# Gated window attention and router: attention product as fp32 32x32 tiles, mask on VectorE, shift on GpSimd, float32r router

## The reference

```python
q = Wq @ layernorm(x) + bq;  k = Wk @ ctx + bk;  v = Wv @ ctx + bv
dots = einsum('bhdt,bhdtw->bhtw', qh, k_win) * 32 ** -0.5   # keys t-8 .. t+7
out = einsum('bhtw,bhdtw->bhdt', softmax(dots), v_win)
x = x + tanh(g_xattn) * (Wo @ out + bo)
# router over the T axis: flat has 16*256 rows of 2048
scores = softmax(flat @ router_weight.T + router_bias)      # 64 experts
topk_w, topk_idx = top_k(scores, 8)
x = x + tanh(g_ffn) * (flat * topk_w.sum() + w_dense @ expert_bias)   # flat = layernorm(x)
```

## Time and profile before

| | us |
|---|---|
| median of 3 runs | 1553.32 (1553.09 to 1555.07) |
| the profiled execution, its own time | 1557.26 |
| its span, first to last instruction | 1555.1 |
| PE busy | 1464.6 (94%) |
| DVE busy | 1276.5 (82%) |
| ACT busy | 1144.8 (74%) |
| POOL busy | 1148.0 (74%) |

### The profile page before, as it was taken

One profiled execution on the slowest core, in us unless ns is written; L12 is line 12 of the kernel. 1 busy time (PEld: TensorE's weight loads), 2 busy tenths in 40 slices (PEclk: granted clock), 3 DMA queues, 4 the chain that ended last, 5 costly groups with the idle time before them and its releaser, 6 DMA issues.

```text
span 1555.1 us, 66658 instructions
## 1 busy us (share of the span) xinstructions
PE 1464.6 (94%) x28162; PEld 1199.9 (77%) x28162; DVE 1276.5 (82%) x2970; ACT 1144.8 (74%) x2009; POOL 1148.0 (74%) x1110
## 2 busy tenths in 40 slices
PE   4799999999999999999999999999999999999985
PEld 3687887888787888878788788878888887778764
DVE  5578987888898887988888898888889888788764
ACT  4687877777787877788787877778787787767652
POOL 4688777787777877877787887778778777677661
PEclk8899999999999999999999999999999999899896
DMA  7455455445546554454555545455554545434132
GB/s 230 125 140 126 106 173 131 123 149 143 147 121 172 141 131 146 121 157 128 149 149 141 156 119 159 128 146 147 144 159 114 159 132 142 121 98 128 44 81 85
DMA packets 365577, 210.39 MB, mean 135 GB/s; under 512 B 294497, under 2 KB 295521, under 8 KB 361057
## 3 DMA queue, kind: packets, MB, share of 16 engines
q1 hardware_dynamic: 365280, 206.14, 49.1%
HBM read 136.88 MB, written 33.55 MB: 110 GB/s over the span
## 4 chain that ended last, share of the span: by engine, by line
PE 46%; DVE 35%; issue 8%; POOL 5%; ACT 3%; DMA 2%; SPq 1%; POOLq 0%; DVEq 0%; ACTq 0%
PE ps_j L1117 18%; PE ps_s L1177 7%; PE ps_a L1142 6%; PE ps_r L1219 5%; DVE prob_t L900 5%; PE ps_s L1117 3%; DVE p_sum L890 3%; DVE st_x L907 2%; DVE wq_lo L822 2%; POOL prob L493 2%; DVE lg L1046 2%; DVE st_in L804 2%; DVE v_turn L871 2%; PE ps_s L1172 2%; PE ps_a L1196 2%
## 5 line engine op out<-in xcount | busy, mean ns | idle before, releaser
L486 POOL TENSOR_TENSOR score<-score,p_inv 128x384 f32<-128x384 f32 x256 | 221.6, 866 | 119.5 <-DVE p_inv L894 117.0
L493 POOL TENSOR_TENSOR prob<-score,prob 128x384 f16<-128x384 f32 x256 | 266.0, 1039 | 38.8 <-ACT prob L644 38.3
L1177 PEld LDWEIGHTS ps_s<-kv_win,q_col 32*32 32x32 f32 x16384 | 198.0, 107 | 57.8 <-issue 57.8
L1177 PE MATMUL ps_s<-kv_win,q_col 32*32 32x48 f32 x16384 | 234.1, 205 | 2.4 <-issue 2.2
L900 DVE STREAM_TRANSPOSE prob_t<-prob 128x512 f32<-128x512 f32 x256 | 176.7, 699 | 55.1 <-POOL prob L493 54.9
L467 POOL TENSOR_TENSOR c_lo<-c_in,c_hi 128x1024 fp32r<-128x1024 f32 x64 | 152.7, 2386 | 89.5 <-ACT c_hi L618 89.5
L1142 PEld LDWEIGHTS ps_a<-prob_t,v_diag 128*128 128x128 f16 x6528 | 175.3, 98 | 50.1 <-DVE prob_t L900 32.6
L1142 PE MATMUL ps_a<-prob_t,v_diag 128*128 128x48 f16 (+2 forms) x6528 | 187.6, 183 | 26.2 <-DVE prob_t L900 19.4
L462 POOL TENSOR_TENSOR att_lo<-att,att_hi 128x512 fp32r<-128x512 f32 x128 | 161.8, 1275 | 51.5 <-ACT att_hi L604 50.3
L1117 PE MATMUL ps_j<-c_hi,wkv_hi 128*128 128x512 f32 x512 | 171.3, 416 | 19.6 <-DVE kv_win L864 10.6
L890 DVE TENSOR_REDUCE p_sum<-score 128x8 f32<-128x384 f32 x256 | 139.2, 544 | 54.3 <-ACT score L638 53.6
(11 more groups left out here) (149 smaller groups left out, 3318.0 us busy)
## 6 DMA issues: line engine op xcount, KB each, us to landing
v_diag<-v_turn SPq DMA_DIRECT2D x512, 68.0 KB, 2.8
c_in<-ctx_dram SPq DMA_DIRECT2D x64, 512.0 KB, 4.9
x_in<-x_dram SPq DMA_DIRECT2D x64, 512.0 KB, 5.5
x_res<-x_dram SPq DMA_DIRECT2D x64, 512.0 KB, 4.3
out_dram<-x SPq DMA_DIRECT2D x32, 1024.0 KB, 7.0
c_sq<-ctx_dram SPq DMA_DIRECT2D x60, 512.0 KB, 5.5
x<-ctx_dram SPq DMA_DIRECT2D x4, 512.0 KB, 6.1
x<-experts_dram SPq DMA_DIRECT2D x2, 512.0 KB, 10.6
```

What stands on the lines that cost most here:

```text
L486: pool.tensor_tensor(score[:, u], score[:, u], p_inv[:, u, :].unsqueeze(2).to_broadcast([P, HALF, KEYS]), ALU.mult).then_inc(pm_rdy, 1)
L493: pool.tensor_tensor(part(prob[:, u % 2], 1)[:, :, 0:KEYS], score[:, u], part(prob[:, u % 2], 0)[:, :, 0:KEYS], ALU.subtract).then_inc(pl_ ...
L1177: ins = pe.matmul(s[head(h), n * KEYS:(n + 1) * KEYS], q_col[head(h), g, at:at + SUB], kv_win[c % 2][head(h), 0, g, at:at + KEYS], start=F ...
```

## The change

- **Attention product.** `attend` takes the turned values `v_turn` and `prob_t` directly, in fp32: for each of 17 blocks four matmuls on four 32x32 tiles, 68 for a group. `v_diag`, its DMAs, the fp16 halves (`high`, `low`, `values_low`) and the bound with its squares, loads and scales are gone. `v_turn` has two buffers.
- **Mask and shift.** The mask matmul is gone. VectorE adds the mask while it reads the scores from PSUM (`masked`), takes the maximum from SBUF, and GpSimd subtracts it (`shift`).
- **Router.** `wr_both` holds high and low part of the router weights as 128 float32r weight columns; the turned rows are split into `turn_hi` (ScalarE) and `turn_lo` (VectorE, `turned_low`) and are the moving operand, 256 columns. Once a sequence the sums are copied out (`logit_sums`), and two fp32 matmuls with `fold` add the halves and turn them back. `wd` and `lg` lie in PSUM.
- The low part of the scaled Wq moves from VectorE to GpSimd; the output is stored in four parts instead of one; the loads at the start stand in another order (no context squares, x ahead of the weights of the router and the experts); the order on each engine is another.

```diff
             def step(b, c, par):
-                if live(b, c, 0):
-
-                    turned, freed = nth(b, c, 0), nth(b, c, -1)
-                    for g in range(G):
-                        need(sp, vt_rdy[g], turned)
-                        need(sp, av_mm[g], freed)
-                        for h in range(HPG):
-                            sp.dma_start(v_diag[head(h), g, :, head(h)],
-                                         v_turn[head(h), g].rearrange("p (j d) -> p j d", d=SUB)).then_inc(vd_ld[g], 16)
...
-                def low(u):
-
-                    need(pool, ph_rdy, done(UNITS, b, c, 0, u))
-                    pool.tensor_tensor(part(prob[:, u % 2], 1)[:, :, 0:KEYS], score[:, u],
-                                       part(prob[:, u % 2], 0)[:, :, 0:KEYS], ALU.subtract).then_inc(pl_rdy, 1)
+                def shift(u, off):
+
+                    rows = score[:, u, :, 0:KEYS]
+                    need(pool, mx_rdy[u], nth(b, c, off))
+                    pool.tensor_tensor(rows, rows, neg_max[:, u, :].unsqueeze(2).to_broadcast([P, HALF, KEYS]),
+                                       ALU.add).then_inc(sh_rdy[u], 1)
...
+                def queries_weight_low():
+
+                    need(pool, wqh_rdy, b + 2)
+                    pool.tensor_tensor(wq_lo[:], wq_ln, wq_hi[:], ALU.subtract).then_inc(wql_rdy, 1)
...
-                def high(u):
-
-                    need(act, pm_rdy, done(UNITS, b, c, 0, u))
-                    need(act, pt_rdy, done(UNITS, b, c, 0, u - 2))
-                    act.activation(part(prob[:, u % 2], 0)[:, :, 0:KEYS], score[:, u], ACT.Copy).then_inc(ph_rdy, 1)
...
+                def logit_sums():
+
+                    need(act, r_mm, nth(b, c, -2))
+                    act.activation(acc[:], ps_r[:, ACC], ACT.Copy).then_inc(acc_rdy, 1)
...
-                def values_low(g):
-
-                    rows = kv_win[c % 2][:, 1, g, OWN]
-                    need(dve, vh_rdy[g], nth(b, c, 2))
-                    dve.scalar_tensor_tensor(part(rows, 1), ps_j[g][:], v_bias[parity(c, 2, par)][:, g:g + 1],
-                                             part(rows, 0), ALU.add, ALU.subtract).then_inc(vl_rdy[g], 1)
+                def masked(u, off):
+
+                    need(dve, s_mm[u], nth(b, c, off))
+                    need(dve, pt_rdy[u], nth(b, c, off - 1))
+                    dve.tensor_tensor(score[:, u, :, 0:KEYS], ps_s[u % 2][:, 0:HALF * KEYS].rearrange("p (n k) -> p n k", k=KEYS),
+                                      mask[:].unsqueeze(1).to_broadcast([P, HALF, KEYS]), ALU.add).then_inc(mk_rdy[u], 1)
...
+                def turned_low(g, off):
+
+                    need(dve, xth_rdy[g], nth(b, c, off))
+                    need(dve, r_mm, nth(b, c, off - 1))
+                    dve.tensor_tensor(turn_lo[:, :, g], ps_t[:].rearrange("p (k t) -> p k t", k=TB), turn_hi[:, :, g],
+                                      ALU.subtract).then_inc(xtl_rdy[g], 1)
...
-                        for n, (kv, kp) in enumerate(((0, 0), (1, 0), (0, 1))):
-                            ins = pe.matmul(ps_a[g][:, q0:q1], part(v_diag[:, g, j], kv),
-                                            part(prob_t[:, g, lo:hi], kp),
-                                            start=(j == 0 and n == 0), stop=(j == NB), skip_group_check=True)
+                        for h in range(HPG):
+                            ins = pe.matmul(ps_a[g][head(h), q0:q1], v_turn[(c + off) % 2][head(h), g, j * SUB:(j + 1) * SUB],
+                                            prob_t[head(h), g, lo:hi],
+                                            start=(j == 0), stop=(j == NB), skip_group_check=True)
...
-                    pe.matmul(s[:, 0:HALF * KEYS], ident_b[:], mask[:].rearrange("p n k -> p (n k)"),
-                              start=True, stop=False, skip_group_check=True)
...
                     for k in range(TB):
-                        for g in range(G):
-                            ins = pe.matmul(ps_r[:, g * E:(g + 1) * E], x1_t[:, g, k], wr[:, ch * TB + k],
-                                            start=(ch == 0 and k == 0 and g == 0),
-                                            stop=(ch == NCH - 1 and k == TB - 1), skip_group_check=True)
+                        for n, v in enumerate((turn_hi, turn_lo)):
+                            ins = pe.matmul(ps_r[:, ACC], wr_both[:, ch * TB + k], v[:, k].rearrange("p g c -> p (g c)"),
+                                            start=(ch == 0 and k == 0 and n == 0),
+                                            stop=(ch == NCH - 1 and k == TB - 1 and n == 1))
...
+                def fold_logits():
+
+                    need(pe, acc_rdy, b)
+                    if b == 1:
+                        need(pe, fold_rdy, 1)
+                    for g in range(G):
+                        ins = pe.matmul(wd[:, g], acc[:, g * P:(g + 1) * P], fold[:],
+                                        start=(g == 0), stop=(g == G - 1), skip_group_check=True)
+                    ins.then_inc(fo_mm, 1)
```

1117 lines of the change are left out of this document (511 added, 606 removed).

## The result

The changed kernel takes **1728.33 us** (median of 4, 1726.16 to 1730.52) where the kernel before takes 1554.01: a ratio of 1.1116, with a 95% interval of 1.1094 to 1.1138. It is 11% slower. The forecast was 1494 us. Of the cases in the prediction it is rival 5, instruction supply, which had 4% and a time of 1750.

What follows compares the result with a forecast made beforehand. PE, busy 94%, was taken to bound the kernel by the sum of its pieces; steps -28, late steps -12, start -18 and end -1 gave -59 from the 1553.32 median: 1494 us, range 1460 to 1540.

Steps and rivals of the forecast that it cites:

- rival 5: Instruction supply: PE gets only 74 instructions per us in the dense stretch; steps grow 4 us, total 1750; chance 4%.
- PE bounds the kernel, and its pieces can be summed: PE's pieces, summed start to start, set the time; a c = 0 step falls 0.66 us to 20.26.
- entry into the tiles: On PE, going from full matmuls to 32x32 tiles costs 0.08 us each time.
- The diagonal's 8 DMAs go, and nobody waits for them any more.: The eight DMAs a step that filled the diagonal disappear; no size was given.
- Rival 4: VectorE full at c = 1, late transposes, PE's clock falls; once per sequence +90, 1584 us; chance 10%.
- Late steps, -12 us: In steps like 57, VectorE's `nt_x` no longer meets GpSimd's `c_lo`; -12 us, bounds -14 and 0.
- Start, -18 us: Less data ahead of x: statistics end near 16, first queries at 25.5; -18 us, bounds -24 and -8.
- The end, -1,: At the kernel's end the last store is only a quarter; -1 us.
- VectorE and GpSimd below PE: VectorE falls from 1276 to 1229 us, below PE on the mean; GpSimd stays unchanged with 26% to spare.
- Wait for the output projection, 0.3 a step: Behind the second product PE has less cover and waits for `att_lo`; 0.3 us a step, between 0 and 0.58.

Runs made afterwards that it cites:

- e10: Changed kernel with the ctx load moved later in the step and the residual and stores ahead of the x load, nothing left out: 1606.34 us.
- e12: Changed kernel with the product reading only the upper 16 bits of values and probabilities, and its loads moved away from the dense part: 1481.00 us.
- e8: As e7, with one matmul a block in the product instead of three, low 16 bits left out: 1511.79 us.
- e7: Changed kernel with the product taken back to 51 full matmuls from the DMA-filled diagonal, low halves left out: 1499.03 us.
- e3: Changed kernel with the steady loads of ctx, x and the residual cut to 32 of 512 columns: 1608.75 us.
- e9: As e3, with one keys projection moved behind the next step's first product and one values projection ahead of the third scores unit: 1724.89 us.

## Why the prediction was wrong

- **PE bounds the kernel, and its pieces can be summed.** Right for the pieces, wrong as a bound. The product takes 1.52 us (828.25 to 829.77) where 1.72 was forecast: 11 ns a pass, not the 12.7 of the scores. The router starts at 835.60 and the scores at 836.75, 1.15 instead of 0.94 and 0.08 for the entry. The scores keep their 0.81. The entry into the tiles costs the 0.08 forecast: 0.54 from 855.48 to 856.02, of which the pair takes 0.46. The sum of the pieces was even 0.3 a step too high. But an undisturbed step hardly exists: the mean of 48 steps in the middle is 26.1 us against 22.9 before, where the forecast's (90.83 - 1.8) / 4 is 22.3; and the median with c = 0 is 25.7 against 20.9, where 20.3 to 20.7 was forecast.
- **The step that failed** is the first conclusion, that the time is set by the sum of PE's pieces: the supply of instructions stood in that sum at nothing. It was named as rival 5, priced at 4 us a step, 1750 in all, and given 4%. In its place the runs show 206 us more lost at blocks and 143 more at the lower clock. That the total comes so near to 1750 is in part luck: a mean step is 3.8 us above the forecast, but the rival knew only the rate of 74 per us, and with the loads out of the way (e10, 1606 us) a step is only 1.7 above it; the loads and the clock, which it left out, make up the rest. The only number beside the rival that speaks for its low chance is that the queue was busy for 1.0% of the time. That is the share of 16 engines' time that transfers take; it says nothing of how soon the next one can follow. 223 blocks in 1555 us are one in 7.0 us on the mean, and 256 instructions of the dense part, at 74 per us or more, need one in 3.5. The smallest distance between two transfers could have been taken from the trace of before: it is 3.28 us there. That one number would have shown that 74 per us is near a limit, and not only a rate that happened to be seen.
- **The page cited beside rival 5.** The Trainium skill (Runtime: NRT & Kernel Launch, Instruction fetch mechanics) gives PE a store of 2048 instructions and calls the cost of a block's boundary mostly hidden. The traces do not agree: when PE enters a block, never more than one further block of 256 has been transferred in any kernel here, and 225 us are lost at boundaries. The measurement decides. What the same section says of blocks of 256, and that the store is only two lines of 16 KiB, the traces bear out.
- **"The diagonal's 8 DMAs go, and nobody waits for them any more."** True, and the second miss. Nobody waited for them, but the ctx load stood behind them in SyncE's queue, and was late by it, 11.7 us into a step. Without them it runs beside the dense part. e10, which moves it back and the residual a little, takes 122 us back.
- **Rival 4, a fall of the clock**, came as a companion and not in the step with c = 1 alone: 233 us at the lower level instead of 90. Its own cause, the wait for the turned probabilities, did not come: 3.6 us are left of the 19.4 of the earlier trace rows.
- **Late steps, -12 us**: right in its mechanism. No `nt_x` was held by GpSimd; the mean of 48 equals the 161 ns of the free ones, where one took 2.20:

```profile
L719 DVE TENSOR_TENSOR nt_x<-nt_x,half_x 128x2 f32<-128x2 f32 x48 | 7.7, 161 | 1.7
```

- **Start, -18 us**: mis-sized at the place that it names. The aggregate of the statistics, at 31.34 before, comes at 14.27, where 16 was said, but the first queries come at 34.09, not 25.5. The 12.2 us that the kernel before needed between them became 19.8, since PE waits until 27.37 for the low part of the second ctx chunk, whose load SyncE issues only at 15.39, behind those of the experts. The first scores start at 38.90 instead of 49.67, 11 us earlier. The first product starts at 51.07 instead of 70.73, 20 us earlier, since the kernel before waited 6.14 us for `q_col` behind its first scores; that this is near the 18 forecast is luck. **The end, -1,** went the other way: from the first product of the last chunk on, the changed kernel takes 46.2 us where the kernel before took 39.4. PE waits there for `turned_low`, which stands behind the last statistics on VectorE, and `fold` comes on top.

```profile
27.37 1.22 PE L994 MATMUL ps_j<-c_hi,wkv_hi 128*128 128x512 f32 x2 [8.74 <-POOL c_lo L447]
...
34.09 0.62 PE L994 MATMUL ps_s<-x_hi,wq_hi 128*128 128x512 f32 x2
```

- **VectorE and GpSimd below PE**: right, 1158 us (1229 forecast) and 1095 (1148 before). **Wait for the output projection, 0.3 a step**: 0.8 us in all; the stops gave ScalarE and GpSimd more time than they needed. A wait appears in another place once the stops go: `turned_low` in front of the transposes and the router, over 100 us in e12 and e8.
- **Without the supply** the rest of the change does give what was forecast in kind, not in size: e7, without the low halves, is 55 us faster than before, where mask, router, start and late steps were forecast at over 100.

What stays open: what makes the clock fall. It is not the time lost at blocks alone: e3 loses 153 us there, in stops of at most 2.4 us, and runs no longer at the lower level (87 us) than the kernel before (90), while the changed kernel with stops of up to 4.7 us runs 233. Open too are some 30 us of what e9 takes over e3. That full operands can be had at the price of e12, with loads moved and `turned_low` earlier, was not tried.

## What to carry to other kernels

Count a kernel's instructions per us in its densest stretch of some 256 to 1000, not on the mean, and set that beside the smallest distance between two transfers of the instruction queue in the trace: here PE got at most some 75 per us once the block at hand was used up (its quickest 960 instructions in a row took 10.2 us, since one block lay ready), and splitting a full matmul into many small tiles ran into it. A wait "<-issue" in the middle of a run of equal matmuls, always at the same number in a block of 256, was the sign of it. Before an unwaited DMA is removed, look at what stands behind it in its queue: the loads that then start earlier may meet the stretch in which PE needs its instructions, and moving one load by 8 us and another by 3 was worth 122 us here.

## What was not expected of the hardware

- Instructions reach PE in blocks of 256 (16 KB), never more than one beyond the block that PE enters: in the 16 kernels here the starts of two transfers are never less than 3.22 us apart, each takes 1.0 us, PE goes on 1.4 us after the end, and every stop over 0.5 us without a semaphore wait is at number 193 of a block.
- Data DMAs delay them: 1.13 us from the request to the start without data, 1.81 with 12 or more engines busy, over 3.2 in a tenth of these cases. The time of request is inferred from PE's position, not recorded.
- A wait on a semaphore that was passed long ago costs 38 ns on the mean between the matmuls of a projection (386 us for 10240).
- An fp32 pass on a 32x32 tile with up to 48 columns takes 11.2 ns in the product (1.52 us for 136) and 12.7 in the scores, one of bf16 9.7 (0.66 us for 68).
- 4352 matmuls fewer gained nothing in e8 (13 us slower than e7, with 105 us more at 1.2 GHz).
